# The order of TensorE's three jobs in a tile: scores, projection, values in place of scores, values, projection

## The chip, the cores and the metric

The kernel runs on one NeuronCore of a Trainium2 chip. The metric is the device time of one execution in microseconds; below it is the median of three runs, and one further execution was profiled.

## What is computed

One layer of a perceiver block on 64 latent rows of width 256. A context of 6272 rows is read by cross attention with 32 heads of width 8, whose queries and keys are normalised by head; then come self attention with weights given as codes and scales, and a mixture of eight experts. The part around the change is the cross attention:

```python
q = x @ Wq.T
k_raw = context @ Wk.T
v_raw = context @ Wv.T
...
q = _rmsnorm(q)
k = _rmsnorm(k)
scale = HEAD_DIM ** (-0.5)
scores = jnp.einsum('bhnd,bhmd->bhnm', q, k) * scale
attn = jax.nn.softmax(scores, axis=-1)
out = jnp.einsum('bhnm,bhmd->bhnd', attn, v)
```

## The kernel before, in words

The context is cut into 49 tiles of 128 rows. Every engine runs its own queue, written out by hand, and they meet by counting semaphores. `steps` (L92) calls each engine's `step` once for a tile number c from -6 to 49: eight numbers ahead of a hardware loop, 40 in the loop (five turns of eight, with waits against a register's value), eight behind it. What an engine does in step c belongs to different tiles, since the work is pipelined: PROJ = 5 steps ahead for the projection, KV = 4 for its normalisation, TR = 3 for the last part of the keys, and PV = -1 for the values. In step t of the steady state:

- **TensorE** (L745): *scores* of tile t in two halves of eight matmuls (L726), each half into two PSUM banks; *values* of tile t-1 in two halves of eight matmuls (L740; each runs as two instructions, so the profile counts 32); *projection* of tile t+5, six matmuls of 512 columns (L762) into one of two banks `ps_kv`. Three terms of split numbers stand in place of one full-precision product.
- **ScalarE** (L405): exponentials of the first half of tile t's scores (L402), squares of the projected keys of tile t+4 (L414), exponentials of the second half (L402), then logarithm and exponential that make the inverse norms of tile t+4 (L420, L424).
- **VectorE** (L527): `ctx_hi` of tile t+6 (L535), the sums of squares of tile t+4 (L541), its values copied out of PSUM (L546), its normalised keys `k_n` (L554, which counts `kn_done`), and the cast that makes the first two parts of these keys (L562).
- **GpSimd** (L350): `ctx_lo` of tile t+6 (L356), the third part of the keys of tile t+3 (L362), and in every third step one `dequantise` (L348) of the self attention's weights.
- **SyncE** loads the context, turns the finished keys by a transposing DMA into `kT` (L280) and loads the weights of the later stages.

The waits of TensorE are these. Scores of tile t wait for the keys of tile t in `kT`, and each half for the exponentials of the same half of tile t-1, whose PSUM banks it overwrites. Values of tile t-1 wait for the exponentials of that tile and its copied values. The projection of tile r = t+5 waits for three counts: `ctx_lo` of tile r, and, since bank r mod 2 was last used by tile r-2, the copied values (`v_done`) and the normalised keys (`kn_done`) of tile r-2 = t+3. That is the tile which ScalarE and VectorE normalise in step t-1. In turn, exponentials wait for scores and for the values of tile t-2, and VectorE's copy of the values (L546) waits for the values of tile t-2 as well (`pv_done`).

Of the kernel before, what the change touches and what calls it, by code (L numbers as in the profile page):

```python
# [91 lines left out]
def steps(engine, body, after):  # L92


    for c in range(FIRST, LOOP0):
        body(Tile(None, c))
        if c in after:
            after[c]()
    with engine.Fori(0, ITERS) as i:
        for j in range(U):  # L100
            body(Tile(i, LOOP0 + j))
    for c in range(LOOP1, LAST + 1):
        body(Tile(None, c))


def wait(engine, semaphore, count):

    if count is not None:
        engine.wait_ge(semaphore, count)


def perceiver(nc, x, ctx_t, xwq, xwkv, codes, scales, wo_scales, qkv_bias, bo, gate_w, gate_bias,
              shared_gw, shared_dw, up_w, down_w, eye, expert_ids, pair_heads, out):
    with ExitStack() as stack:
# [562 lines left out]
        def _(pe):  # L677
# [38 lines left out]
            def scores(t, half):  # L716


                if half == 0:
                    pe.wait_ge(keys_in[t.slot(4)], t.landed())  # L720
                wait(pe, exp_done, t.count(2, half - 1))
                for k in range(PAIRS // 2):
                    r = half * PAIRS // 2 + k
                    e, at = k % 2, k // 2 * P
                    rows = slice(e * RT, e * RT + PR)
                    last = nc.tensor.matmul(ps_scores[half][:, e, at:at + P], kT[rows, t.slot(4), r // 2],  # L726
                                            q_blk[rows, r // 2].rearrange("p h n -> p (h n)"), start=(k < 2),
                                            stop=(k >= PAIRS // 2 - 2), skip_group_check=True)
                last.then_inc(scores_mm, 1)

            def values(t, half):

                wait(pe, exp_done, t.count(2, half + 1))
                if half == 0:
                    wait(pe, v_done, t.count(plus=1))
                for k in range(PAIRS // 2):
                    r = half * PAIRS // 2 + k
                    j, g = r % CG, r // CG
                    at = k % 2 * 512 + k // 2 * P
                    last = nc.tensor.matmul(ps_o[CT * j:CT * j + VW, g * P:(g + 1) * P], v_sb[:, t.slot(8), r],  # L740
                                            probs[:, t.slot(2), half, at:at + P], start=False,
                                            stop=False, skip_group_check=True)
                last.then_inc(pv_done, 1)

            def step(t):  # L745
                pv, kv = t.ahead(PV), t.ahead(PROJ)
                for half in range(2):
                    if t.exists():
                        scores(t, half)
                for half in range(2):  # L750
                    if pv.exists():
                        values(pv, half)
                if kv.exists():

                    wait(pe, ctx_lo_done, kv.count(plus=1))
                    wait(pe, v_done, kv.count(plus=-1))
                    wait(pe, kn_done, kv.count(plus=-1))
                    a = kv.slot(2)
                    terms = [(lhs[:, a, c], rhs[:, c]) for c in range(DC)
                             for lhs, rhs in ((ctx_hi, wkv_hi), (ctx_hi, wkv_lo), (ctx_lo, wkv_hi))]  # L760
                    for n, (lhs, rhs) in enumerate(terms):
                        last = nc.tensor.matmul(ps_kv[a], lhs, rhs, start=(n == 0), stop=(n == len(terms) - 1))  # L762
                    last.then_inc(kv_mm, 1)

            steps(pe, step, {-4: queries_mm, -2: queries_turned})

            pe.wait_ge(ready("o_sb"), 1)
# [170 lines left out]
```

## Time and profile before

| What | us |
|---|---|
| Median of 3 runs | 259.95 |
| Lowest and highest | 259.41, 262.91 |
| The profiled execution's own time | 261.99 |
| Its span, first to last instruction | 260.2 |
| TensorE busy in the span | 230.8 |
| ScalarE, VectorE, GpSimd busy | 144.6, 139.7, 106.5 |

Engines in the profile: PE is TensorE's matmuls, PEld its weight loads, DVE VectorE, ACT ScalarE, POOL GpSimd, SPq the DMA issues of SyncE. Each row of a timeline gives the start in the span, the duration, the engine, the line and what is written and read; matmuls of one job that follow each other are merged into one row (x16 for scores, x32 for values). The end of a matmul is modelled and overlaps the next one, so times of TensorE are taken from start to start. A job is named by its line: L726 scores, L740 values, L762 projection.

### The profile page before, as it was taken

To read this page: it belongs to the slowest core of one execution; us is meant where nothing else is said; L and a number is where in the kernel's file an instruction comes from. 1 tells how busy PE (TensorE), PEld (TensorE's weight loads), DVE (VectorE), ACT (ScalarE), POOL (GpSimd) and SP (SyncE) were. 2 spreads that over 40 slices of the span, in tenths; PEclk is the share of its full clock that TensorE was granted. 3 is DMA by queue.
4 is the path that set the end of the run, shared out by engine and by line. 5 is a ranking of instruction groups with operands and counts; after the bars stand their busy time and mean duration, and the time that the engine had idled before them with its cause. 6 is when DMAs were issued, how large, how long until landed. Compare 5 with 4: busy or idle time off the path is not lost.

```text
span 260.2 us, 7971 instructions
## 1 busy us (share of the span) xinstructions
PE 230.8 (89%) x3030; PEld 161.8 (62%) x3030; DVE 139.7 (54%) x355; ACT 144.6 (56%) x278; POOL 106.5 (41%) x124
## 2 busy tenths in 40 slices
PE   0676999999999999999999999854799999749995
PEld 0444777777777777777777777533667867424463
DVE  3476566766775776776676676304213341354630
ACT  2032988888888888888888888952002021121200
POOL 3225465866766676577576586450000000000000
PEclk9997999999999999999999999989569999977999
DMA  6219999999998999998799999999930000000000
GB/s 188 90 34 216 229 177 202 173 242 230 224 196 202 212 210 212 204 224 199 185 239 216 217 243 171 243 261 295 254 90 0 3 0 0 0 3 0 0 0 10
DMA packets 68186, 39.63 MB, mean 152 GB/s; under 512 B 53993, under 2 KB 62985, under 8 KB 68169
## 3 DMA queue, kind: packets, MB, share of 16 engines
q1 hardware_dynamic: 67800, 39.34, 67.2%
q8 instruction: 10, 0.16, 0.3%
q10 hardware_dynamic: 368, 0.07, 0.1%
q14 instruction: 8, 0.06, 0.1%
HBM read 26.48 MB, written 0.07 MB: 102 GB/s over the span
## 4 chain that ended last, share of the span: by engine, by line
PE 83%; DVE 7%; DMA 5%; issue 2%; ACT 2%; POOL 1%; SPq 0%; DVEq 0%; ACTq 0%
PE ps L762 29%; PE ps L740 18%; PE ps L726 10%; PE ps L690 9%; PE ps L788 7%; DMA kT<-k 3%; PE ps L870 3%; PE ps L832 2%; DMA wkv_f<-xwkv 2%; PE ps L815 2%; PE ps L824 1%; PE ps L866 1%; PE ps L799 1%; DVE k_n L554 1%; DVE wkv_lo L488 0%
## 5 line engine op out<-in xcount | busy, mean ns | idle before, releaser
L402 ACT ACTIVATE room<-ps 128x1024 f32<-128x1024 f32 x98 | 100.3, 1029 | 23.7 <-PE ps L726 23.7
L356 POOL TENSOR_TENSOR ctx_lo<-ctx_f,ctx_hi 128x256 fp32r<-128x256 f32 x49 | 35.9, 733 | 61.3 <-DVE ctx_hi L535 61.3
L740 PE MATMUL ps<-room,v_flat 128*17 128x128 f32 x1568 | 53.2, 278 | 0.0
L762 PE MATMUL ps<-wkv_hi,ctx_hi 128*128 128x512 f32 x98 | 44.9, 458 | 4.4 <-DVE q_blk L524 2.4
L740 PEld LDWEIGHTS ps<-room,v_flat 128*17 128x17 f32 x1568 | 39.2, 98 | 5.4 <-issue 0.2
L762 PE MATMUL ps<-wkv_hi,ctx_lo 128*128 128x512 f32 x98 | 39.7, 405 | 0.0
L762 PE MATMUL ps<-wkv_lo,ctx_hi 128*128 128x512 f32 x98 | 39.5, 403 | 0.0
L562 DVE CAST k<-k_n 128x512 f16<-128x512 f32 x49 | 36.8, 752 | 2.6
L348 POOL TENSOR_TENSOR w_all<-w_all,s_ring 128x1024 f32<-128x1024 f32 x16 | 38.0, 2373 | 0.4 <-DMA s_ring<-wo_scales 0.4
L726 PEld LDWEIGHTS ps<-q_blk,kT 48*128 48x128 f16 x784 | 22.7, 96 | 22.3 <-issue 13.7
L726 PE MATMUL ps<-q_blk,kT 48*128 48x128 f16 x784 | 31.7, 221 | 3.9 <-DMA kT<-k 2.7
L362 POOL TENSOR_TENSOR k<-k_n,k 128x256 f16<-128x256 f32 x49 | 33.1, 675 | 4.2 <-DVE k L562 4.2
L554 DVE TENSOR_TENSOR k_n<-ps,k_r 128x256 f32<-128x256 f32 x49 | 20.8, 425 | 25.0 <-ACT k_r L424 25.0
L541 DVE TENSOR_REDUCE k_ss<-k_sq 128x32 f32<-128x256 f32 x49 | 20.4, 415 | 20.0 <-ACT k_sq L414 19.9
L762 PEld LDWEIGHTS ps<-wkv_hi,ctx_hi 128*128 128x128 f32 x98 | 19.0, 193 | 17.4 <-issue 10.6
L414 ACT ACTIVATE k_sq<-ps 128x256 f32<-128x256 f32 x49 | 18.5, 377 | 7.9 <-PE ps L762 7.9
L762 PEld LDWEIGHTS ps<-wkv_hi,ctx_lo 128*128 128x128 f32 x98 | 19.0, 193 | 4.7
L762 PEld LDWEIGHTS ps<-wkv_lo,ctx_hi 128*128 128x128 f32 x98 | 19.2, 196 | 2.4
L546 DVE COPY v_flat<-ps 128x256 f32<-128x256 f32 x49 | 20.2, 412 | 0.0
L420 ACT ACTIVATE k_ln<-k_ss,eps_rms 128x32 f32<-128x32 f32 x49 | 16.1, 328 | 5.9 <-DVE k_ss L541 5.7
L788 PE MATMUL ps<-hT,w_all 128*128 128x64 f32 x128 | 18.4, 313 | 0.4 <-DVE hT L585 0.4
L788 PEld LDWEIGHTS ps<-hT,w_all 128*128 128x128 f32 x128 | 17.8, 227 | 1.4 <-issue 0.8
(114 smaller groups left out, 163.6 us busy)
## 6 DMA issues: line engine op xcount, KB each, us to landing
w_all<-codes SPq DMA_DIRECT2D x16, 512.0 KB, 4.2
ctx_f<-ctx_t SPq DMA_DIRECT2D x49, 128.0 KB, 2.9
s_ring<-scales SPq DMA_DIRECT2D x12, 256.0 KB, 4.0
up_sb<-up_w SPq DMA_DIRECT2D x8, 352.0 KB
s_ring<-wo_scales SPq DMA_DIRECT2D x4, 512.0 KB, 5.2
dn_sb<-down_w SPq DMA_DIRECT2D x8, 176.0 KB
kT<-k SPq DMA_TRANSPOSE x49, 3.6
sgw_sb<-shared_gw SPq DMA_DIRECT2D x1, 704.0 KB, 4.7
```

Source lines behind the costliest of these rows:

```text
L348: nc.gpsimd.tensor_tensor(w, w, s, ALU.mult).then_inc(ring_free[u % RING], 1)
L356: nc.gpsimd.tensor_tensor(ctx_lo[:, split.slot(2)], ctx_f[:, split.slot(4)], ctx_hi[:, split.slot(2)].bitcast(F32), ALU.subtract).then_inc ...
L362: nc.gpsimd.tensor_tensor(key_part(keys, 2), k_n[:, keys.slot(2)].rearrange("p (r h d) -> p r h d", h=2, d=XD), key_part(keys, 0), ALU.sub ...
L402: nc.scalar.activation(probs[:, t.slot(2), half], ps_scores[half].rearrange("p b n -> p (b n)"), ACT.Exp).then_inc(exp_done, 1)
L541: nc.vector.tensor_reduce(k_ss[:, r.slot(2)], k_sq[:, r.slot(2)].rearrange("p (h d) -> p h d", d=XD), AX_X, ALU.add).then_inc(ss_done, 1)
L554: nc.vector.tensor_tensor(kn, ps_kv[r.slot(2)][:, 0:D].rearrange("p (h d) -> p h d", d=XD), k_r[:, r.slot(2)].unsqueeze(2).to_broadcast([P ...
L562: nc.vector.tensor_copy(key_parts(r)[:, :, :, 0:2, :], pairs.unsqueeze(3).to_broadcast([P, PAIRS, 2, 2, XD])).then_inc(k1_done, 1)
L690: last = nc.tensor.matmul(dst, hT[:, c, :], rhs(c), start=(c == 0), stop=(c == DC - 1))
L726: last = nc.tensor.matmul(ps_scores[half][:, e, at:at + P], kT[rows, t.slot(4), r // 2], q_blk[rows, r // 2].rearrange("p h n -> p (h n)") ...
L740: last = nc.tensor.matmul(ps_o[CT * j:CT * j + VW, g * P:(g + 1) * P], v_sb[:, t.slot(8), r], probs[:, t.slot(2), half, at:at + P], start= ...
L762: last = nc.tensor.matmul(ps_kv[a], lhs, rhs, start=(n == 0), stop=(n == len(terms) - 1))
L788: last = nc.tensor.matmul(ps[:, g % 2, (w * GH + h) * N:(w * GH + h + 1) * N], w_all[:, 3 * g + w, at:at + SD], hT[:, c, :], start=(c == 0 ...
```

## The change

TensorE's `step` issues the projection between the scores and the values; before it stood behind the values. The waits go with the instructions that they belong to, and no other engine's queue is touched. What was S(t) V(t-1) P(t+5) becomes S(t) P(t+5) V(t-1), with S, V and P for scores, values and projection.

```diff
                 for half in range(2):
                     if t.exists():
                         scores(t, half)
-                for half in range(2):
-                    if pv.exists():
-                        values(pv, half)
                 if kv.exists():
 
                     wait(pe, ctx_lo_done, kv.count(plus=1))
...
                     last.then_inc(kv_mm, 1)
+                for half in range(2):
+                    if pv.exists():
+                        values(pv, half)
```

TensorE's queue in one step of the loop before (names in brackets are the semaphores that an instruction waits for; REGISTER_ALU computes a count to wait for):

```order
L726 MATMUL ps<-q_blk,kT 128x128 x7
L740 MATMUL ps<-room,v_flat 17x128 [waits v_done,exp_done]
L740 MATMUL ps<-room,v_flat 17x128 x7
L740 MATMUL ps<-room,v_flat 17x128 [waits exp_done]
L740 MATMUL ps<-room,v_flat 17x128 x7
L109 REGISTER_ALU
L762 MATMUL ps<-wkv_hi,ctx_hi 128x512 [waits kn_done,v_done,ctx_lo_done]
```

The same place in the changed kernel, where the projection is L759:

```order
L726 MATMUL ps<-q_blk,kT 128x128 x7
L109 REGISTER_ALU
L759 MATMUL ps<-wkv_hi,ctx_hi 128x512 [waits kn_done,v_done,ctx_lo_done]
L759 MATMUL ps<-wkv_lo,ctx_hi 128x512
L759 MATMUL ps<-wkv_hi,ctx_lo 128x512
L759 MATMUL ps<-wkv_hi,ctx_hi 128x512
L759 MATMUL ps<-wkv_lo,ctx_hi 128x512
L759 MATMUL ps<-wkv_hi,ctx_lo 128x512
L109 REGISTER_ALU [waits exp_done]
L740 MATMUL ps<-room,v_flat 17x128 [waits v_done]
```

The projection's first matmul, with its three waits, has moved from behind 16 matmuls of values to directly behind the last scores; the values follow it.

TensorE's queue in step 1 before, the last one ahead of the loop that is filled with all three jobs:

```order
L726 MATMUL ps<-q_blk,kT 128x128 [waits exp_done,keys_in1]
L726 MATMUL ps<-q_blk,kT 128x128 x7
L726 MATMUL ps<-q_blk,kT 128x128 [waits exp_done]
L726 MATMUL ps<-q_blk,kT 128x128 x7
L740 MATMUL ps<-room,v_flat 17x128 [waits v_done,exp_done]
L740 MATMUL ps<-room,v_flat 17x128 x7
L740 MATMUL ps<-room,v_flat 17x128 [waits exp_done]
L740 MATMUL ps<-room,v_flat 17x128 x7
L762 MATMUL ps<-wkv_hi,ctx_hi 128x512 [waits kn_done,v_done,ctx_lo_done]
```

And in the changed kernel:

```order
L726 MATMUL ps<-q_blk,kT 128x128 [waits exp_done]
L726 MATMUL ps<-q_blk,kT 128x128 x7
L759 MATMUL ps<-wkv_hi,ctx_hi 128x512 [waits kn_done,v_done,ctx_lo_done]
L759 MATMUL ps<-wkv_lo,ctx_hi 128x512
L759 MATMUL ps<-wkv_hi,ctx_lo 128x512
L759 MATMUL ps<-wkv_hi,ctx_hi 128x512
L759 MATMUL ps<-wkv_lo,ctx_hi 128x512
L759 MATMUL ps<-wkv_hi,ctx_lo 128x512
L740 MATMUL ps<-room,v_flat 17x128 [waits v_done,exp_done]
L740 MATMUL ps<-room,v_flat 17x128 x7
```

Here the projection of tile 6 has moved ahead of the values of tile 0. In the steps without scores or values (ahead of step 0) and without a projection (behind step 43) the queue is what it was.

## Rows read from the trace of the kernel before

**Rows 1.** Busy time by stretch: us, then each engine's busy us; clock, DMA share, GB/s
```profile
30.00:163.00 133.00, 133.00 (x2273) 96.38 (x2273) 90.65 (x210) 113.06 (x213) 90.21 (x99) 1.00 0.98 210
163.00:178.00 15.00, 10.83 (x273) 7.92 (x272) 2.68 (x7) 10.18 (x13) 6.01 (x4) 0.89 1.11 259
```

**Rows 2.** Groups by line, 30 to 163 us; the last column is idle time before them
```profile
L402 ACT ACTIVATE room<-ps 128x1024 f32<-128x1024 f32 x85 | 87.5, 1030 | 18.4 <-PE ps L726 18.4
...
L762 PE MATMUL ps<-wkv_hi,ctx_hi 128*128 128x512 f32 x85 | 38.0, 447 | 0.0
...
L348 POOL TENSOR_TENSOR w_all<-w_all,s_ring 128x1024 f32<-128x1024 f32 x14 | 33.3, 2376 | 0.0
```

**Rows 3.** Timeline, 84.3 to 91 us: start us, us, engine, line, what [idle before <-releaser]
```profile
83.89 2.37 POOL L348 TENSOR_TENSOR w_all<-w_all,s_ring 128x1024 f32<-128x1024 f32 x1
...
84.38 0.62 PE L726 MATMUL ps<-q_blk,kT 48*128 48x128 f16 x16
...
85.01 1.53 DVE L562 CAST k<-k_n 128x512 f16<-128x512 f32 x1
...
87.52 0.62 PE L726 MATMUL ps<-q_blk,kT 48*128 48x128 f16 x16
...
87.73 0.42 DVE L554 TENSOR_TENSOR k_n<-ps,k_r 128x256 f32<-128x256 f32 x1 [0.32 <-ACT k_r L424]
87.96 1.02 ACT L402 ACTIVATE room<-ps 128x1024 f32<-128x1024 f32 x1 [0.27 <-PE ps L726]
...
88.07 1.07 PE L740 MATMUL ps<-room,v_flat 128*17 128x128 f32 x32
...
88.89 0.74 POOL L356 TENSOR_TENSOR ctx_lo<-ctx_f,ctx_hi 128x256 fp32r<-128x256 f32 x1 [0.69 <-DVE ctx_hi L535]
89.07 0.19 PEld L762 LDWEIGHTS ps<-wkv_hi,ctx_hi 128*128 128x128 f32 x1 [0.21 <-issue]
89.07 0.50 PE L762 MATMUL ps<-wkv_hi,ctx_hi 128*128 128x512 f32 x1
...
90.34 0.40 PE L762 MATMUL ps<-wkv_hi,ctx_lo 128*128 128x512 f32 x1
...
90.66 0.39 PEld L726 LDWEIGHTS ps<-q_blk,kT 48*128 48x128 f16 x14 [0.37 <-issue]
...
90.68 0.42 DVE L554 TENSOR_TENSOR k_n<-ps,k_r 128x256 f32<-128x256 f32 x1 [0.64 <-ACT k_r L424]
```

**Rows 4.** Timeline, 43.3 to 50.5 us: another tile behind a stretched cast
```profile
46.58 0.62 PE L726 MATMUL ps<-q_blk,kT 48*128 48x128 f16 x16
...
49.77 0.42 DVE L554 TENSOR_TENSOR k_n<-ps,k_r 128x256 f32<-128x256 f32 x1 [0.32 <-ACT k_r L424]
```

**Rows 5.** Timeline, 109.5 to 113.3 us: a tile with later keys
```profile
109.54 0.62 PE L726 MATMUL ps<-q_blk,kT 48*128 48x128 f16 x16
...
112.78 0.42 DVE L554 TENSOR_TENSOR k_n<-ps,k_r 128x256 f32<-128x256 f32 x1 [0.55 <-ACT k_r L424]
```

**Rows 6.** Timeline, 27.6 to 31.5 us: the step with the first values
```profile
27.70 0.62 PE L726 MATMUL ps<-q_blk,kT 48*128 48x128 f16 x16
...
28.28 0.42 DVE L554 TENSOR_TENSOR k_n<-ps,k_r 128x256 f32<-128x256 f32 x1 [0.63 <-ACT k_r L424]
...
29.25 0.50 PE L762 MATMUL ps<-wkv_hi,ctx_hi 128*128 128x512 f32 x1
```

**Rows 7.** Timeline, 163.3 to 168.3 us: scores released by exponentials
```profile
163.44 1.02 ACT L402 ACTIVATE room<-ps 128x1024 f32<-128x1024 f32 x1 [0.46 <-PE ps L726]
...
164.61 0.40 PE L726 MATMUL ps<-q_blk,kT 48*128 48x128 f16 x8
164.62 1.03 ACT L402 ACTIVATE room<-ps 128x1024 f32<-128x1024 f32 x1
...
165.71 0.40 PE L726 MATMUL ps<-q_blk,kT 48*128 48x128 f16 x8 [0.70 <-ACT room L402]
```

**Rows 8.** The chain that ended last, in order of time
```profile
164.68 7.33 DMA kT<-k
```

## The prediction

> **What bounds the kernel now.** I read the busy times by stretch first, then the groups by line, then the timeline. From 30 to 163 us TensorE is busy for all 133 of 133 us at a granted clock of 1.00, its 2.4 GHz level, while ScalarE has 113, VectorE 91 and GpSimd 90 us of work [rows 1]. No group of matmuls there has idle time before it, while ScalarE waits 18.4 us for scores [rows 2]. So TensorE sets the pace of the 43 tiles in the middle, and no wait of its own is behind it. The timeline shows one tile [rows 3]: scores at 87.52, values at 88.07, projection at 89.07, next scores at 90.66. That is 0.55 + 1.00 + 1.59 = 3.14 us, and the same from 84.38 to 87.52. The busy TensorE is not one at its peak: its weight loads sat idle 0.21 us ahead of the projection and 0.37 us ahead of the scores, since each job begins its loads only about 0.07 us before the modelled end of the last matmul of the job before: 88.14, 89.14 and 90.74 against loads or matmuls at 88.07, 89.07 and 90.66.
>
> The question is therefore twofold: does a tile's work on TensorE get longer or shorter in the new order, and does a wait that has room today lose it.
>
> **What the change leaves alone.** Number and shape of the matmuls stay, and so do all queues but TensorE's. Of the borders between jobs there are three in a tile before and after. What a job costs at its end is the running out of its own last matmul (0.40 us recorded for the projection's, less its streaming), and what it costs at its start is its own first weight load. On that reading the three borders cost the same in either order, and a tile stays at 3.14 us: term 0. The stretch has no border from scores to projection, so the term has bounds. Below: the load of 0.19 us that opens the projection [rows 3] vanishes. Above: the dearest idle before a load now, 0.37 us, replaces the cheapest, which would be some 0.1 to 0.2 us a tile.
>
> The trace shows no load of one job begun before the end of the other's matmuls, with the three pairs of numbers above. The Trainium skill (TensorEngine Tiling (Array Packing), Key Properties) says that a change of tiling mode drains TensorE; scores use pairs of 48 rows, values groups of 17 columns, and the projection the whole array, so each border is such a change, and by that rule the term is 0. The Trainium skill also says (TensorE: Matmul & The Clock Gate, Part 2, what each phase is for) that a weight load is pulled ahead of matmuls in flight when row groups don't conflict or when it goes to the background buffer; by that the projection's first load could hide under the scores. The trace speaks for the first.
>
> The values now end right ahead of the next scores, later by a projection. Who waits for them? The exponentials of tile t wait for the values of t-2, which end at about the start of scores t plus 0.07 us; the exponentials start 0.44 us after the scores do (87.52 to 87.96, rows 3), on the scores' account. 0.37 us are left, and VectorE's copy comes later still: cost 0.
>
> **What the change adds.** The projection in step t+1 waits for the normalised keys (`kn_done`) that are made from tile t's step. Before, it stands 0.55 + 1.00 us behind the start of scores t+1; after it, only 0.55 us behind. So it is wanted 3.14 + 0.55 = 3.69 us after the start of scores t. When are the keys there?
> - Ordinary tile [rows 3]: scores 87.52, keys end 90.68 + 0.42 = 91.10, which is 3.58 behind.
> - A tile whose keys are late by the next exponentials: 109.54, end 113.20, 3.66 behind [rows 5]. By my reading of the timeline about one tile in four is like this.
> - A tile behind a dequantisation. GpSimd's product of 2.37 us lies over VectorE's cast, which then takes 1.53 us (83.89 and 85.01 in rows 3), and all that follows is late: 84.38 to 88.15, 3.77 behind; in the lightest such tile 46.58 to 50.19, 3.61 behind [rows 4]. 14 of the 43 tiles (L348 x14) [rows 2]; half way between is 3.69.
>
> To that comes what passes between the end of the keys and the start of the matmul. Two rows measure it on TensorE [rows 7]: exponentials end at 163.44 + 1.02 = 164.46 and scores that wait for two counts start at 164.61, 0.15 later; exponentials end at 165.65 and scores with one wait start at 165.71, 0.06 later. The projection waits for three counts; I take 0.15. So an ordinary projection is late by 3.58 + 0.15 - 3.69 = 0.04, the second kind by 0.12, the third by 0.15 (0.07 to 0.23). TensorE has no slack, so lateness is lost. But a projection that is late by d moves the following scores by d, and the next projection is wanted d later while its keys (from the scores before) are not: what one loses is deducted from the next. In a group of three tiles the one behind the dequantisation loses 0.15 - 0.04 = 0.11, the next nothing, the third 0.04. That is 0.15 us in three tiles, and 14 x 0.15 = 2.1 us.
>
> Once there is more. In step 1 scores start at 27.70 behind a quicker step, and the keys end at 28.28 + 0.42 = 28.70 [rows 6]. The projection, at 29.25 before, is wanted at 28.25 and can start at 28.85: 0.60 us lost.
>
> `ctx_lo` keeps its room: the one of rows 3 ends at 89.63, and the projection that reads it is wanted at 90.66 + 0.55 = 91.21 or later. Behind the waiting projection TensorE's queue holds the values and the next scores, and for these wait the exponentials; that is how the loss reaches all engines. The end of the stage follows the last scores with projection as before: the chain there runs through the keys' transposing DMA of 7.33 us [rows 8], issued from work that is timed by the scores. It is moved, not covered: nothing given back.
>
> **Sum.** 0 + 2.1 + 0.6 = +2.7 us. On the profiled execution's 261.99 us (span 260.2) that is 264.7; that execution is 2.0 above the median of 259.95, within the runs' 259.41 to 262.91, and the kernel's own difference carries over: 259.95 + 2.7 = 262.65, rounded 262.7, or 1.0% slower, which is less than the 2% or so that a measurement of this kernel tells from no change. Bounds of the wait's term: with 0.06 us in place of 0.15, ordinary tiles lose nothing, the third kind some 0.05, and step 1 0.5: +1.2. The other end is the nearest long interval that the trace has between a keys' end and the projection, 28.70 to 29.25, 0.55 us. With it every projection is late, and each by half of 3.63 + 0.55 - 3.69, as the deduction halves it: 0.245 x 42 + 1.0 = +11.3. In the trace this interval is filled by the values' matmuls, so I stay by 0.15.
>
> **Rivals.**
> - *The projection's wait is dear (slower).* Place: the first matmul of each projection in the loop, where counts are computed in registers next to the wait. For it: three waits where 0.15 was measured with two, and everything behind the waiting instruction is held as well. Against it: the counts are computed ahead, under the scores. Price: half of (3.63 + l - 3.69) a tile, with l the time from keys to matmul, plus 0.46 + l once. It passes 2% (5.2 us) from l = 0.29 on. At l = 0.35: 0.145 x 42 + 0.8 = 6.9 us, 266.9.
> - *The projection's weights load under the scores (faster).* It saves 0.19 us a tile at most on TensorE; but now the keys bound the pace: two tiles can't be shorter than keys 3.64 + wait 0.15 + projection and values 2.59 - 0.19 = 6.19 us, 3.10 a tile. So it wins 0.04 to 0.05 us x 42 = 1.9, and step 1 costs 0.4: 258.5. (This is what the Trainium skill's rule on weight loads, TensorE: Matmul & The Clock Gate, Part 2, would do here.) This ring is also why I give little to a gain over 2%: 5.2 us would need 3.02 us a tile.
> - *Nothing comes late.* Keys move with the exponentials; if these ran earlier against the scores the lateness would vanish but for step 1: +0.6, 260.6. Nothing in the change makes them earlier.
>
> **Chances.** Forecast (late keys, +1.2 to +4.5) 0.66; dear wait 0.14; loads hidden 0.08; nothing late 0.09; some gain over 2% that I don't see 0.03. The range reaches from the loads-hidden case to just under the dear wait: 259.0 to 266.0. Faster by over 2%: 0.03; slower by over 2%: 0.12, since a part of the dear wait falls short of it; within: 0.85.
>
> **What would show it.** In the profile after, between 30 and 163 us, the projection follows 0.55 us behind the scores in most tiles and 0.6 to 0.8 us behind after a stretched cast, with idle time of TensorE put down to `k_n` (L554); the step from scores to scores is 3.14 us in ordinary tiles and up to 3.3 in those. In step 1 the projection starts near 28.85 and the scores of tile 2 near 31.4. The three borders add up to the same idle time of the loads. Wrong it is if scores to scores differs from 3.14 in tiles without a wait (border term), if the projection starts over 0.25 us behind the keys in most tiles (dear wait), or if the keys end less than 3.5 us behind the scores.

## The result and the profile after

The changed kernel takes 264.06 us in the median (263.33 to 264.69, 6 runs) against 259.9 (259.27 to 262.91, 6 runs): ratio 1.0144, with a 95% interval of 1.0093 to 1.0194. It is slower, by less than 2%. Here and below, medians are of all runs of a kernel, while ratios leave out the runs that took over 1.5% longer than that kernel's fastest. The profiled execution took 263.33 us, with a span of 261.5.

What answers to [rows 2] in the changed kernel, the groups by line from 31 to 161 us (the projection is line 759 here; the last column is idle time before them):

```profile
L402 ACT ACTIVATE room<-ps 128x1024 f32<-128x1024 f32 x82 | 84.4, 1030 | 19.3 <-PE ps L726 19.3
L740 PE MATMUL ps<-room,v_flat 128*17 128x128 f32 x1320 | 44.2, 274 | 0.0
L759 PE MATMUL ps<-wkv_hi,ctx_hi 128*128 128x512 f32 x82 | 35.7, 435 | 0.5
L348 POOL TENSOR_TENSOR w_all<-w_all,s_ring 128x1024 f32<-128x1024 f32 x14 | 33.4, 2384 | 0.0
```

And the waits ahead of TensorE's weight loads in the same stretch (engine and line, what is waited for: us in total, times, longest us):

```profile
PEld ps L740 <- issue: 15.0, 41, 0.4
PEld ps L726 <- issue: 8.8, 42, 0.2
PEld ps L759 <- issue: 1.8, 9, 0.3
```

The projection's matmuls had no idle time before them and now have 0.5 us. The second table tells where one job hands over to the next. Ahead of the values the loads sit idle for 15.0 / 41 = 0.37 us, ahead of the scores for 8.8 / 42 = 0.21 us. Before it was 0.37 us ahead of the scores and 0.21 us ahead of the projection [rows 3]. So the idle time belongs to the job that leaves, 0.37 us behind a projection and 0.21 us behind values, and what comes next doesn't change it. The third row, ahead of the projection, is idle time in nine tiles only, where the projection waited for late keys.

Now three tiles of the changed kernel in the timeline (start us, us, engine, line, what, idle before):

```profile
81.77 0.62 PE L726 MATMUL ps<-q_blk,kT 48*128 48x128 f16 x16
81.78 0.42 DVE L554 TENSOR_TENSOR k_n<-ps,k_r 128x256 f32<-128x256 f32 x1 [0.63 <-ACT k_r L424]
...
82.35 0.47 PE L759 MATMUL ps<-wkv_hi,ctx_hi 128*128 128x512 f32 x1
...
84.91 0.62 PE L726 MATMUL ps<-q_blk,kT 48*128 48x128 f16 x16
...
88.13 0.62 PE L726 MATMUL ps<-q_blk,kT 48*128 48x128 f16 x16
88.27 0.42 DVE L554 TENSOR_TENSOR k_n<-ps,k_r 128x256 f32<-128x256 f32 x1 [0.32 <-ACT k_r L424]
...
88.81 0.19 PEld L759 LDWEIGHTS ps<-wkv_hi,ctx_hi 128*128 128x128 f32 x1 [0.23 <-issue]
88.84 0.47 PE L759 MATMUL ps<-wkv_hi,ctx_hi 128*128 128x512 f32 x1
...
89.38 0.19 PEld L759 LDWEIGHTS ps<-wkv_hi,ctx_hi 128*128 128x128 f32 x1
...
91.28 0.42 DVE L554 TENSOR_TENSOR k_n<-ps,k_r 128x256 f32<-128x256 f32 x1 [0.63 <-ACT k_r L424]
...
91.39 0.45 PEld L726 LDWEIGHTS ps<-q_blk,kT 48*128 48x128 f16 x16 [0.21 <-issue]
91.40 0.62 PE L726 MATMUL ps<-q_blk,kT 48*128 48x128 f16 x16
...
91.95 0.50 PE L759 MATMUL ps<-wkv_hi,ctx_hi 128*128 128x512 f32 x1
```

First tile: scores at 81.77, keys end at 81.78 + 0.42 = 82.20, projection at 82.35, that is 0.15 us behind the keys and 0.58 us behind the scores, 0.03 us later than TensorE itself would have it. Yet the tile takes 84.91 - 81.77 = 3.14 us as before. Second tile, behind a stretched cast: scores at 88.13, keys end at 88.69, projection at 88.84, again 0.15 us behind the keys, but 0.71 us behind the scores; the tile takes 3.27 us. Third tile: keys end at 91.70, only 0.30 us behind the scores, since the scores themselves were put off by the projection before; the projection starts at 91.95, 0.55 us behind the scores, and waits for nothing. This is the pattern that was forecast, lateness of one deducted from the next.

In 37 of the 41 tiles of the loop the projection starts 0.14 to 0.16 us behind the end of its keys.

How it adds up, with times read from the timelines (us; each is the start of the scores of that tile):

| Profile | tile 0 | tile 2 | tile 43 | tile 48 | last instruction | loop: 2 to 43 |
|---|---|---|---|---|---|---|
| Before | 24.92 | 30.85 | 159.86 | 173.98 | 260.2 | 129.0 |
| After | 24.57 | 31.09 | 160.94 | 173.46 | 261.5 | 129.9 |

The loop has lost 0.85 us. At tile 48 the changed kernel is 0.5 us *ahead*, and then it loses 1.8 us in stages that the change doesn't touch. One profile of each can't say what of that is the change's.

### The profile page after: what moved, and what is told of

It reads as the page before. It is cut to its first block, busy times and chain, and to the rows that moved or that the text cites. A ratio compares the mean times of both kernels' runs of the same rounds, so it can differ in the third digit from the quotient of the medians.

```text
span 261.5 us, 7971 instructions
## 1 busy us (share of the span) xinstructions
PE 233.6 (89%) x3030; PEld 162.5 (62%) x3030; DVE 139.0 (53%) x355; ACT 144.3 (55%) x278; POOL 106.7 (41%) x124
## 4 chain that ended last, share of the span: by engine, by line
PE 79%; DVE 7%; issue 4%; DMA 4%; ACT 4%; POOL 1%; SPq 1%; DVEq 0%; ACTq 0%
PE ps L759 27%; PE ps L740 16%; PE ps L690 10%; PE ps L726 9%; PE ps L788 7%; PE ps L832 3%; DMA kT<-k 3%; PE ps L870 3%; PE ps L815 2%; ACT room L402 1%; PE ps L824 1%; DMA x_sb<-x 1%; DVE h_sb L473 1%; PE ps L866 1%; POOL ctx_lo L356 1%
## 5 line engine op out<-in xcount | busy, mean ns | idle before, releaser
L740 PEld LDWEIGHTS ps<-room,v_flat 128*17 128x17 f32 x1568 | 38.6, 97 | 17.7 <-issue 16.4
L759 PE MATMUL ps<-wkv_hi,ctx_hi 128*128 128x512 f32 x98 | 44.1, 450 | 4.9 <-DVE q_blk L524 2.4
L759 PE MATMUL ps<-wkv_hi,ctx_lo 128*128 128x512 f32 x98 | 40.0, 408 | 0.0
L759 PE MATMUL ps<-wkv_lo,ctx_hi 128*128 128x512 f32 x98 | 39.8, 406 | 0.0
L759 PEld LDWEIGHTS ps<-wkv_hi,ctx_hi 128*128 128x128 f32 x98 | 19.1, 195 | 13.9 <-issue 3.3
L759 PEld LDWEIGHTS ps<-wkv_hi,ctx_lo 128*128 128x128 f32 x98 | 19.1, 195 | 4.7
L759 PEld LDWEIGHTS ps<-wkv_lo,ctx_hi 128*128 128x128 f32 x98 | 19.3, 197 | 2.5
```

## The experiments

Twelve kernels, on three chips. The measured times of the kernel before spread more there (258.9 to 266.7 us) than in the first comparison (259.3 to 262.9), so the ratios carry intervals of 0.3 to 1.0% to each side, and the sharp instrument is the loop's length in the profile. It was 129.0 us in both profiles of the kernel before and 129.9 in both of the changed one.

### Both kernels again

> The kernel before again, unchanged, as a control with a second profile. Every theory: ratio 1.00 within 0.5%. From the scores of tile 2 to the scores of tile 43 (the loop) 129.0 us, as in the first profile. What the two profiles differ by behind the loop (the keys' transposing DMA, the granted clock) is what one execution differs from another by, and no difference of that size between two kernels' single profiles counts.

> The changed kernel again, unchanged. Late keys: about 1.014 of the kernel before, and scores of tile 2 to scores of tile 43 again about 129.9 us, 0.8 over the kernel before. If that holds, 0.8 us of some 4 are explained in the loop, and the rest lies ahead of or behind it: either in the first two tiles (0.6 us forecast) and at the end of the cross attention, or in the clock of the later stages.

The kernel before: 261.83 us, ratio to itself 0.9997 (0.9927 to 1.0066); loop 129.02 us. The changed kernel: 263.94 us, ratio 1.0048 (1.0013 to 1.0083), and not 1.014; loop 129.87 us. The loop's 0.85 us is therefore firm, and it is far less than the 4.2 us by which the medians of the first comparison differ. The start of the changed kernel's control is this:

```profile
24.89 1.04 PE L726 MATMUL ps<-q_blk,kT 48*128 48x128 f16 x16
...
27.74 0.62 PE L726 MATMUL ps<-q_blk,kT 48*128 48x128 f16 x16
...
28.25 0.42 DVE L554 TENSOR_TENSOR k_n<-ps,k_r 128x256 f32<-128x256 f32 x1 [0.63 <-ACT k_r L424]
...
28.82 0.47 PE L759 MATMUL ps<-wkv_hi,ctx_hi 128*128 128x512 f32 x1 [0.46 <-DVE k_n L554]
...
30.39 1.07 PE L740 MATMUL ps<-room,v_flat 128*17 128x128 f32 x32
...
31.39 0.62 PE L726 MATMUL ps<-q_blk,kT 48*128 48x128 f16 x16
```

Scores of tile 1 start at 27.74, the keys end at 28.25 + 0.42 = 28.67, and the projection, wanted at 28.29, starts at 28.82, with 0.46 us of idle time put down to `k_n`. From the scores of tile 0 to those of tile 2 it takes 6.50 us against 5.93 before (24.92 to 30.85), in two profiles whose clock was low in nearly the same place, the scores of tile 0 and the first third of the projection of tile 5: 0.57 us, where 0.60 was forecast. In the first profile of the changed kernel the low clock lasted through most of the projection of tile 5, which put off the scores of tile 1, and the projection of tile 6 was hardly late (0.57 behind them); the same stretch took 6.52 us. The 0.57 us is one pair's, though. In the order of before the stretch took 5.93, 5.62 and, where the clock was low longest, 6.65 us (the kernel before, its control and the kernel with the loads moved, below), while four profiles of the changed order, wherever their clock was low, gave 6.49 to 6.52. What the start costs thus depends on the clock.

Behind the loop two profiles of one and the same kernel can differ by more than the change costs in the loop. From the scores of tile 43 to those of tile 48 it is 14.1 and 13.0 us before, 12.5 and 15.9 us after. The longest of these is a wait for the last keys but one:

```profile
169.42 0.40 PE L726 MATMUL ps<-q_blk,kT 48*128 48x128 f16 x8 [0.42 <-ACT room L402]
...
174.38 1.04 PE L726 MATMUL ps<-q_blk,kT 48*128 48x128 f16 x16 [3.56 <-DMA kT<-k]
```

From there to the end it is 86.2 and 86.1 us before, 88.0 and 86.5 after, and the granted clock goes with it (us of the stretch, busy us of each engine, then granted clock, DMA share, GB/s; the kernel before and the changed one, first profiles):

```profile
174.00:260.00 86.00, 72.77 (x453) 48.26 (x449) 29.57 (x89) 13.31 (x30) 0.00 (x0) 0.89 0.20 56
```

```profile
173.50:261.50 88.00, 74.33 (x450) 48.52 (x449) 29.50 (x89) 12.88 (x29) 0.42 (x1) 0.84 0.21 62
```

The matmuls are the same, at a mean granted clock of 0.89 and of 0.84.

### Two theories of the border: values on both sides

```diff
+                if pv.exists():
+                    values(pv, 0)
                 if kv.exists():
...
-                for half in range(2):
-                    if pv.exists():
-                        values(pv, half)
+                if pv.exists():
+                    values(pv, 1)
```

> Order scores, first half of values, projection, second half of values: the projection is wanted 0.5 us later than in the changed kernel, so no keys are late. Late keys: the projection starts about 1.05 us behind the scores, no wait on k_n, scores to scores 3.14 us in all tiles if a fourth border costs nothing (both halves of values have one shape, so there are four borders in place of three); by the drain theory the fourth border costs about 0.2 us a tile, so 3.3 us a tile, +8 us in all, 1.03. Rival (border costs follow the pair, not the drain): 3.14 us a tile, ratio 1.00 to 1.005.

267.1 us (4 runs), ratio 1.0179 (1.0075 to 1.0283); loop 134.30 us, 5.3 us over the kernel before. No projection waits: it starts 1.11 or 1.12 us behind the scores in every tile, and in the rows below its first load, at 80.70, follows the first half of the values with 0.21 us of idle time, as any load behind values does. A tile takes 3.27 us, and the fourth border costs 5.3 / 41 = 0.13 us. The rival, by which a tile stays at 3.14 us, falls; the price was put too high by me (0.2). Every border here is also a change of the part of the array that is used, so the runs don't tell which of the two costs.

```profile
80.14 0.63 PE L740 MATMUL ps<-room,v_flat 128*17 128x128 f32 x16
...
80.70 0.19 PEld L761 LDWEIGHTS ps<-wkv_hi,ctx_hi 128*128 128x128 f32 x1 [0.21 <-issue]
80.71 0.50 PE L761 MATMUL ps<-wkv_hi,ctx_hi 128*128 128x512 f32 x1
...
82.30 0.35 PEld L740 LDWEIGHTS ps<-room,v_flat 128*17 128x17 f32 x16 [0.37 <-ACT room L402]
82.30 0.63 PE L740 MATMUL ps<-room,v_flat 128*17 128x128 f32 x16
...
82.89 0.45 PEld L726 LDWEIGHTS ps<-q_blk,kT 48*128 48x128 f16 x16 [0.24 <-issue]
...
83.45 0.63 PE L740 MATMUL ps<-room,v_flat 128*17 128x128 f32 x16
```

Behind the projection it is 0.37 us before a load of the values, as in the changed kernel. The row puts it down to ScalarE, but the exponentials that these values wait for had long been done.

### The keys earlier: ScalarE's squares first

```diff
-                if t.exists():
-                    exps(t, 0)
                 r = t.ahead(KV)
...
                 if t.exists():
+                    exps(t, 0)
                     exps(t, 1)
```

> The changed kernel with ScalarE's squares ahead of both exponentials of a step, where ScalarE sat idle 0.3 us anyway. The keys are then ready about 0.3 us earlier against the scores (3.3 in place of 3.58). Late keys: the projection never waits, scores of tile 2 to scores of tile 43 back to 129.0 us, so 0.8 us less than the changed kernel, and about 1.010 if the rest of the loss lies elsewhere, 1.00 if all of it hangs on late keys. Rival (all of the loss is in the later stages or the start): same ratio as the changed kernel, 1.014.

> The kernel before with the same move of ScalarE's squares. Late keys: nothing to win, since its projection has 1 us of room; scores of tile 2 to scores of tile 43 stay 129.0 us, ratio 1.00. Rival (the earlier squares help by themselves, at the start or the end of the cross attention): it gains as much as the changed kernel with the squares moved did against the kernel before, 0.992.

In the changed order the projection now starts 0.54 to 0.56 us behind the scores in every tile of the loop (in step 1, ahead of it, it still waits and starts 0.76 behind), also in this tile behind a stretched cast, where the projection is line 758:

```profile
87.51 0.42 DVE L553 TENSOR_TENSOR k_n<-ps,k_r 128x256 f32<-128x256 f32 x1 [0.32 <-ACT k_r L423]
87.57 0.62 PE L725 MATMUL ps<-q_blk,kT 48*128 48x128 f16 x16
...
88.12 0.50 PE L758 MATMUL ps<-wkv_hi,ctx_hi 128*128 128x512 f32 x1
```

The keys end at 87.93, 0.19 us ahead of the projection, and the loop is 129.01 us: all of its 0.85 us came from late keys. These rows also settle the rival by which the projection's weights load under the scores: nothing holds this projection, and it starts 0.55 us behind the scores like the values in the order of before, not earlier.

The time is 260.24 us, ratio 0.9924 (0.9875 to 0.9973), below both of the ratios expected (1.010 and 1.00), and 1.2% below the changed kernel's 1.0048, of which the loop is 0.3%. In the order of before the loop stays at 128.95 us, as it should, and the ratio is 0.9911 (0.9852 to 0.9969) where 1.00 was expected. That ratio rests on five of its ten runs against all thirteen of the kernel before; the medians of all are 261.96 and 262.50 us, only 0.2% apart. So a gain of the squares outside the loop is shown in the changed order and not settled in the old one, for which the rival of this pair can't be decided. What the profiles show of it is 0.27 us between the scores of tiles 45 and 46 (2.30 in place of 2.57), in either order; the rest I can't place.

### The keys later: one more exponential

```diff
+                    wait(act, extra_done, r.count(plus=0))
+                    nc.scalar.activation(extra[:], ident[:, 0:XH], ACT.Exp).then_inc(extra_done, 1)
                     nc.scalar.activation(k_ln[:, a], k_ss[:, a], ACT.Ln, bias=eps_rms[:],
```

> The changed kernel with one more small exponential on ScalarE in each tile, of a constant into a tile that nothing reads, between the second exponentials and the inverse norms. It makes each tile's keys later by about 0.26 us against the scores (3.84 in place of 3.58). Late keys with the deduction (what one projection loses the next doesn't): in an ordinary tile 3.84 + 0.15 - 3.69 = 0.30 late, halved 0.15, of which 0.03 are taken up inside the projection: 0.12 us a tile, and from the scores of tile 2 to those of tile 43 134 us (133 to 136). Without the deduction: 0.27 a tile, 140 us. Rival (the projection's wait costs nothing by itself): 129.9.

> The kernel before with the same extra exponential. Its projection is wanted 4.69 us behind the scores, so 3.84 is early; ScalarE still has room. Late keys: 129.0 us from the scores of tile 2 to those of tile 43, as without it. Rival (ScalarE itself is the bound then): over 130.

In the order of before: loop 128.95 us, untouched, 262.75 us in the one run. In the changed order: loop 132.29 us, 266.63 us in the one run. The keys moved by 0.11 us only, not 0.26 (3.69 us behind the scores; the extra instruction overlaps its neighbours), so 134 was too much. The rows show the deduction at work:

```profile
47.75 0.62 PE L731 MATMUL ps<-q_blk,kT 48*128 48x128 f16 x16
47.87 0.42 DVE L559 TENSOR_TENSOR k_n<-ps,k_r 128x256 f32<-128x256 f32 x1 [0.74 <-ACT k_r L429]
...
48.44 0.47 PE L764 MATMUL ps<-wkv_hi,ctx_hi 128*128 128x512 f32 x1
...
51.00 0.62 PE L731 MATMUL ps<-q_blk,kT 48*128 48x128 f16 x16
51.02 0.42 DVE L559 TENSOR_TENSOR k_n<-ps,k_r 128x256 f32<-128x256 f32 x1 [0.54 <-ACT k_r L429]
...
51.59 0.47 PE L764 MATMUL ps<-wkv_hi,ctx_hi 128*128 128x512 f32 x1
...
54.15 0.62 PE L731 MATMUL ps<-q_blk,kT 48*128 48x128 f16 x16
```

Keys end at 48.29, projection at 48.44, 0.69 us behind the scores, and the tile takes 3.25 us; then keys at 51.44, projection at 51.59, 0.59 behind, and the tile takes 3.15. Many tiles go in such pairs, where every other one loses 0.10 us, which is 41 / 2 x 0.10 = 2.1 us over the 129.9 of the changed kernel, 132.0 against the 132.3 measured. Without the deduction each would, 134. The same instruction costs 2.4 us in one order and nothing in the other: that is the slack that the change has used up.

### The stretched cast

```diff
-                    w = w_all[:, u].rearrange("p (c n) -> p c n", c=DC)
-                    s = s_ring[:, u % RING, 0:512].unsqueeze(1).to_broadcast([P, DC, 512])
+                    w = w_all[:, u, 0:32]
+                    s = s_ring[:, u % RING, 0:32]
                 else:
-                    w, s = w_all[:, u], s_ring[:, u % RING]
+                    w, s = w_all[:, u, 0:32], s_ring[:, u % RING, 0:32]
```

> The changed kernel in which each dequantisation multiplies only 32 columns by their scales, so most of the self attention's weights are left as codes; the cast on VectorE is then no longer stretched. Late keys: the losses of tiles behind a stretched cast go, and those of tiles with later exponentials (3.66) stay, about 0.08 us in some five to seven of them: 129.4 to 129.5 us from the scores of tile 2 to those of tile 43, in place of 129.9. Rival (the loss is not of the cast's making): 129.9 unchanged.

Loop 129.35 us (261.66 us in the one run), close to what was expected. So 0.51 us of the loop's 0.85 hang on the dequantisation beside VectorE's cast, and 0.34 on what is left: five tiles, whose exponentials or those before them start 0.52 and not 0.44 us behind the scores, lose 0.06 to 0.10 us each.

### The end of the cross attention: the last loads out of the keys' way

```diff
-                if 0 <= u < UNITS and piece == 0:
+                if 0 <= u < UNITS - 1 and piece == 0:
                     load_codes(u)
-                if 0 <= u < UNITS and piece == 1:
+                if 0 <= u < UNITS - 1 and piece == 1:
                     load_scales(u)
...
+            load_codes(UNITS - 1)
+            load_scales(UNITS - 1)
             for dst, src in large:
```

The two kernels with both moves have the squares' diff as well.

> The kernel before with the loads of the last unit of weights (its codes and scales) issued behind the last keys' transposing DMA, not among the last three. If the last keys land late because these loads lie ahead of them, the scores of tile 43 to those of tile 48 take 11.2 us (3.15 + 1.61 + 2.57 + 2.23 + 1.61, the shortest seen of each) in place of 14.1 and 13.0, and the ratio is about 0.991. Rival (the late landing has another cause, such as the context's loads): 13 to 14 us, 1.00.

> The changed kernel with the same move of the last unit's loads. Late keys alone: 0.85 us in the loop and 0.57 us in the first tiles over the kernel before with that move, 1.4 us or 0.5%, and the same 11.2 us at the end of the cross attention. Rival (the changed order costs more behind the loop, as a ratio of 1.014 in the first comparison would have it): over 3 us more than the kernel before with that move.

> The changed kernel with the last unit's loads moved and the squares ahead of the exponentials. Late keys: loop 129.0 us, so 1.1 us less than the changed kernel with the loads moved, plus 0.3 us at the end (2.30 in place of 2.57 between the scores of tiles 45 and 46); against the kernel before 0.985 to 0.990. Should be the fastest with the changed order.

> The order of before with both moves. Late keys: its loop is 129.0 us as well, so it differs from the changed order with both moves only by the first tiles (5.8 or 5.9 us from the scores of tile 0 to those of tile 2, against 6.2): 0.3 to 0.4 us faster than it, 0.984 to 0.989 of the kernel before. Rival (the changed order has a gain of its own that late keys hid): the changed order with both moves is the faster one.

| Kernel | median us (runs) | ratio to before, 95% | loop | tile 43 to 48 |
|---|---|---|---|---|
| Order before, loads moved | 259.69 (12) | 0.9961, 0.9926 to 0.9996 | 128.95 | 11.6 |
| Order after, loads moved | 261.51 (12) | 1.0002, 0.9969 to 1.0036 | 130.11 | 11.3 |
| Order after, both moves | 260.72 (12) | 0.9957, 0.9916 to 0.9998 | 129.27 | 11.2 |
| Order before, both moves | 259.38 (10) | 0.9937, 0.9897 to 0.9976 | 128.95 | 11.3 |

In the second and the third row one tile near 150 us takes 3.42 and 3.39 us by another wait: the scores behind it stand 0.2 us idle for their keys' transposing DMA. Without it the loops would be those of the changed kernel and of the squares moved, 129.9 and 129.0. The end is 11.2 to 11.6 us in all four, as expected where the loads are to blame. Scores of tile 47 no longer wait for a DMA (order of before with the loads moved; it was idle there for 2.66 and 1.69 us in the two profiles of the kernel before, and for 3.56 us in the control of the changed one):

```profile
168.91 0.40 PE L728 MATMUL ps<-q_blk,kT 48*128 48x128 f16 x8 [0.42 <-ACT room L404]
...
170.23 0.90 PE L728 MATMUL ps<-q_blk,kT 48*128 48x128 f16 x16
```

Yet only about 1 us of the 1.4 to 4.6 arrives in the measured times, and the ratios of about 0.991 and 0.984 to 0.990 that were expected are missed. In the changed order with both moves, 11.2 us in place of 13.1 with the squares alone at this end are followed by 87.8 us in place of 87.0:

```profile
171.20:259.00 87.80, 72.67 (x453) 47.67 (x449) 31.07 (x89) 13.35 (x30) 2.34 (x1) 0.88 0.24 74
```

The row holds what took it: GpSimd has 2.34 us of work there, against 0.00 in the kernel before. The unit whose loads were moved is now multiplied by its scales behind the cross attention, and that product lies over VectorE's addition at its end, first in the kernel before's control, then in the order of before with the loads moved:

```profile
178.51 0.42 DVE L578 TENSOR_TENSOR x<-x_sb,o_cat 64x256 f32<-64x256 f32 x1
```

```profile
177.13 2.34 POOL L350 TENSOR_TENSOR w_all<-w_all,s_ring 128x1024 f32<-128x1024 f32 x1 [6.11 <-DMA s_ring<-wo_scales]
...
177.94 1.81 DVE L580 TENSOR_TENSOR x<-x_sb,o_cat 64x256 f32<-64x256 f32 x1
```

The addition takes 1.81, 1.97, 1.92 and 1.86 us in the four kernels with the loads moved, and 0.42 in all ten other profiles. It stands in the chain that ended last, so the move gives back 1.4 to 1.6 us of what it won. It is the stretched cast again, in a place where nothing covers it.

Between the two orders with the loads moved the medians differ by 1.8 us and the ratios by 0.4%, which is 1.1 us. Forecast from the traces was 1.4. The intervals of the two overlap, so this agrees with the forecast and doesn't prove it; the rival's 3 us and more lie outside. With both moves the ratios differ by 0.2%, in favour of the old order, as expected but inside the noise. The rival, a gain of its own that late keys had hidden, has nothing for it. The old order with both moves is at 0.9937 of the kernel before (0.9897 to 0.9976), faster than the kernel before by more than the noise; whether it is also faster than the squares alone (0.9911, 0.9852 to 0.9969) or slower, the intervals don't tell.

## Why the prediction was right, and where it was off

The sign, the mechanism and the class were right (slower, within 2%, 264.06 us in the range of 259.0 to 266.0). The size was not: the late keys that the prediction names cost about 1.4 us in the traces, where 2.7 were forecast and 4.2 measured. The single terms fared so:

- **The border term, 0: right.** Tiles without a wait take 3.14 us in either order, and the idle times ahead of loads moved with the job that leaves. The rule that a change of tiling mode drains TensorE (the Trainium skill, TensorEngine Tiling (Array Packing), Key Properties) fits this, as it fits the fourth border's 0.13 us; the pull-ahead of loads that the rival was built on was not seen across a border. One reading of the prediction goes too far: its three pairs show loads begun 0.07 us ahead of the modelled end of the last matmul, not behind it, so they show that loads aren't pulled far ahead, and not a full drain.
- **The wait's length, 0.15 us: right.** 82.20 to 82.35, 88.69 to 88.84, 48.29 to 48.44. The dear wait didn't come. (By its own formula it would have passed 2% from 0.27 us on, not 0.29. The range, said to reach down to the loads-hidden case of 258.5, stopped at 259.0.)
- **The loop, 2.1 us: over by a factor of 2.5; measured 0.85.** Three steps of its sum failed. First, "an ordinary projection is late by 3.58 + 0.15 - 3.69 = 0.04" is true, but it costs nothing: a projection that starts 0.58 us behind the scores lasts 1.56 or 1.57 us to the values and not 1.59 or 1.60, which takes up the lateness. That removes the 14 x 0.04 of the third tiles, 0.6 us. Second, the tiles behind a dequantisation were put at 14 x 0.11 = 1.5 us; there are 13 in the loop, they take 0.7 us more than tiles without a wait in both profiles of the changed kernel, and the kernel without the full dequantisation puts 0.51 us of the loop down to it. Taking the middle of the extremes, 3.69, did little harm, for the mean of the 13 is 3.68 in the trace of before. But in the changed kernel the same keys end 3.64 us behind the scores. The cast ends 0.27 to 0.30 us behind the end of GpSimd's product in every profile of either kernel, and this product starts 0.65 us ahead of the next scores in place of 0.59, so its end comes earlier against them. Third, the tiles with later exponentials, "by 0.12", enter no term of the sum; five such tiles cost 0.34 us in the kernel without the full dequantisation. The omission made up for a part of what was too much.
- **Step 1, 0.60 us: right in the control** (0.57; projection at 28.82 against 28.85 forecast). Where the clock is low during most of the projection before, the scores come later by it, the wait for the keys nearly vanishes, and the start takes as long all the same. Against a profile of before with another clock at the start the difference is another: 0.9 us against its control.
- **"It is moved, not covered: nothing given back": not settled.** The end of the cross attention and what follows differ by 3.4 and by 1.5 us between the two profiles of the changed kernel, by the landing of the last keys and with the granted clock, so no single pair of profiles can show it.

The traces show 0.85 + 0.57 = 1.4 us, or 0.55%, the second term from one pair of profiles. The second comparison measured 0.48% (0.13 to 0.83) and the pair with the loads moved some 0.4%; the first measured 1.44% (0.93 to 1.94). The forecast of 2.7 us lies between, but its being near the first is luck in part: the runs of before in the first comparison had a median of 259.9 us, and those of the later comparisons 262 to 263. The 2.8 us between the 1.4 of the traces and the 4.2 of the first comparison have no cause shown. Whether the changed order more often meets the long landing or the low clock, and so costs more than 1.4 us on some chips, was not settled; what would tell is the share of each in many profiles of both kernels.

## What to carry to other kernels

Moving work within a saturated engine's queue gained nothing by itself here: count the borders between kinds of matmuls, which cost by what leaves, and then look at which wait the moved piece is brought nearer to. A buffer that is reused after two tiles makes a ring over two tiles, so a lateness that comes in every tile is lost only by half. Compare the ready time plus the measured wake-up (0.15 us here) with the new start for each kind of tile, give each kind its term in the sum, and expect the ready times to shift a little with the change. Before moving a load out of the way, look at which engine its consumer will then lie over. Where a stage's end hangs on a DMA, take two profiles of the same kernel before reading a difference there.

## What the runs showed of the hardware

A released wait took 0.15 us from the end of VectorE's keys to the matmul that waits for three counts, in every tile looked at (0.14 to 0.16 where it was what held the matmul). A change from one kind of matmul to the next left the weight loads idle for 0.37 us behind fp32 matmuls of 512 columns over the whole array and for 0.21 us behind those of 17 weight columns, whatever followed. The half clock (1.2 GHz) came in stretches that fell differently from execution to execution: a mean granted clock of 0.84 in place of 0.89 in the last 86 to 88 us went with 1.8 us more for the same matmuls. While a GpSimd product of 128x1024 numbers ran, VectorE's work was stretched: a cast from 0.43 to some 1.5 us, ending 0.27 to 0.30 us behind the product, and an addition of 64x256 from 0.42 to between 1.81 and 1.97 us.
